# Four-layer graph network on one core: the second tile's record gather ahead of a semaphore clearing, and the relus of a slab ahead of the copies of the batch in front

## The chip, the cores and the metric

The kernel runs on one core of one Trainium2 chip. The metric is the device time of one execution in microseconds (us), as the median of several runs. Engines are called PE (TensorE; PEld its weight loads), DVE (VectorE), ACT (ScalarE), POOL (GpSimd) and SP (SyncE, which only issues transfers here). Each engine carries out its own instructions in order and waits on semaphores for the others.

## The reference

There are 2048 nodes with 512 features and 67584 edges sorted by destination. Four pre-norm layers are added to x one after another: graph attention with a bias by edge, a three-layer GCN, a single GCN layer, and a weighted sum over edges.

```python
h = relu(layernorm(x));  x = x + attention(h, edges, edge_attr)   # 32 graphs of 64 nodes, 8 heads
h = relu(layernorm(x));  x = x + gcn3(h, edges, W1..W3)
h = relu(layernorm(x));  x = x + gcn1(h, edges, W, b)
h = relu(layernorm(x));  x = x + relu(segment_sum((h @ weight)[dst] * edge_weight, src))
```

The attention needs, for each pair of nodes of a graph, the sum of the biases of the edges between them; the other layers need the counts and the weights of the edges as dense matrices. The change lies in the stage that builds these.

## The kernel before

The program has an edge stage (`edge_prep`, about the first 45 us), a build stage (`build_matrices`, up to about 440 us), the attention, and the three convolutions.

The edge stage packs each edge into a record of 11 fields in DRAM (`rec_dram`), computes the start index of each graph's records, normalizes x, and begins the transfers and projections of the build stage. Its semaphores form one block (`keep.prep`).

The build stage takes the records in 8 tiles (`GTILES`), t = 0 to 7. For each tile POOL issues two indirect transfers, z = 0 and 1, into the one buffer `gathered` (L718; those of tile 0 are at L241). PE transposes the 11 fields (`turn_fields`, L1128), which raises the semaphore `read` by 3 and so frees the buffer. ACT copies the fields from PSUM, DVE makes keys and ACT and DVE make two-part values of them. A tile is worked in 8 batches, so there are 64 batches, n = 8 t + i. Batch n is, engine by engine:

- DVE, `hots(n)`: one-hot matrices by comparison with iotas (L838, L841, L843), products with the weights (L851) and with the biases (L858). DVE works one batch ahead: in iteration n it issues hots(n+1), which waits until the matmuls of batch n-1 are done. In `hots(n+1)` it also issues `h_low` (L785) where batch n has node tiles to turn. Iteration 4 of a tile adds `prep_keys`, iteration 5 `residual` (L776, L777) for the next tile. `weight_low` (L822) makes the low parts of weights in iterations 1 to 3 and later ones.
- PE: the projection pieces that are put into this batch (L1183, L1166, 12 matmuls each), `turn_h` of node tiles (L1149), 32 matmuls for the biases (L1229, needs hots(n)), in the fourth batch of a tile `turn_fields(t+1)` (needs the gather of the next tile), then 32 short matmuls for counts and weights (L1240, L1241), and `turn_weights(n-4)` (L1140).
- ACT: the copies of the pieces, `copy_turned` (L1012) of node tiles, `copy_sums(n)` (L985 bias, fields of the next tile, L992 counts, L999 weights), `copy_weights(n-4)` (L980), parts of weights (`weight_high`, L1038), `relu(t)` (L1003, which reads a node tile of x that SP has loaded), and in the fourth batch of a tile `copy_part` (L967, L968).

Node tiles are turned in pairs, a slab. The first slabs are done at the start of the stage; later pairs are turned in batches 6, 12, 17, 22, 28 and 33. The relus that they need are issued in the batch in front of these: 5, 11, 16, 21, 27 and 32. Which batch holds which pieces is a fixed table (`projections`).

In `build_pool` the gathers of tile t wait for `read` to reach 3 t. Before the gathers of tile 1 POOL calls `clear_prep`, which waits until the last users of the edge stage's semaphores are through (among them `w_high`, raised by the four L1038 of batch 1) and clears them (L730).

Of the kernel before, what the change touches and what calls it, by code (L numbers as in the profile page):

```python
# [579 lines left out]
LAST = GTILES * NBATCH  # L580
# [41 lines left out]
def projections(first_round):  # L622

    pieces = {n: [] for n in range(LAST)}
    if not first_round:
        return pieces
    number, n = 0, SLAB_START  # L630

    def add(place, slab, parts):
        nonlocal number
        for c in parts:
            pieces[place].append(("q" if c < KT else "k", number, slab, c % KT))
            number += 1
    pieces["turns"], pieces["early"], pieces["start"] = [("h", 0), ("h", 1)], [], []
    add("early", 0, (0, 1))
    add("start", 0, (2, 3, 4, 5))
    pieces["start"].append(("total", 0))  # L640
    add(1, 0, (6, 7))
    pieces[1] += [("h", 2), ("h", 3)]
    for slab in range(1, SLABS):
        c = 0
        while c < 2 * KT:
            amount = 2 if slab == 1 else 1 if slab == SLABS - 1 and c >= KT else PIECES_OF_BATCH[n % NBATCH]
            take = range(c, min(c + amount, KT if slab == SLABS - 1 and c < KT else 2 * KT))
            add(n, slab, take)
            c = take.stop
            n += 1  # L650
        if slab + 1 < SLABS:
            pieces[n - 1] += [("h", 2 * slab + 2), ("h", 2 * slab + 3)]
    assert n <= V_START
    assert not any(piece[0] == "q" for b in range(min(b for b in HIGHS if 2 * KT in HIGHS[b]) + 1, V_START) for piece in pieces[b])
    pieces[SECOND_TOTAL].append(("total", 1))
    j, n = 0, V_START
    while j < 2 * NT:
        for _ in range(min(VALUES_OF_BATCH[n % NBATCH], 2 * NT - j)):
            pieces[n].append(("v", number, j // 2, j % 2))
            number += 1  # L660
            j += 1
        n += 1
    assert n < LAST
    return pieces


def work_slots(first_round):


    marks, uses = [], {}  # L670

    def use(key, mark):
        n = len(marks)
        uses[key] = n % WORK, marks[n - WORK] if n >= WORK else None
        marks.append(mark)
    pieces = projections(first_round)

    def use_pieces(place):
        for piece in pieces[place]:
            if piece[0] == "h":  # L680
                use(piece, ("h_copied" if piece[1] < 2 else "h_low", piece[1] + 1))
            elif piece[0] == "total":
                use(piece, ("w_read", 2 * piece[1] + 1))
            else:
                use(piece, ("projected", piece[1] + 1))
    if first_round:
        use_pieces("turns")
        use_pieces("early")
    for f in range(FGROUPS):
        use(("fields", 0, f), ("turned", f + 1))  # L690
    if first_round:
        use_pieces("start")
    for n in range(LAST):
        t, i = divmod(n, NBATCH)
        use_pieces(n)
        if t + 1 < GTILES and i == 3:
            for f in range(FGROUPS):
                use(("fields", t + 1, f), ("turned", FGROUPS * (t + 1) + f + 1))
        if n >= 4:
            use(("chunk", n - 4), chunk_mark(n - 4, first_round))  # L700
    for c in range(LAST - 4, LAST):
        use(("chunk", c), chunk_mark(c, first_round))
    return uses


def build_pool(nc, io, keep, m, s, first_round):

    pool = nc.gpsimd
    records = io["rec_dram"].rearrange("e f -> (e f)").unsqueeze(1)
    if not first_round:  # L710
        pool.wait_ge(s["indexed"], 1)
    for t in range(1 if first_round else 0, GTILES):
        if t > 0:
            pool.wait_ge(s["read"], FGROUPS * t)
        if first_round and t == 1:
            clear_prep(pool, keep, s)
        for z in range(2):
            pool.indirect_dma_start(keep.gathered[:, z, :], None, records,  # L718
                                    bass.IndirectOffsetOnAxis(ap=keep.idx[:, 2 * t + z:2 * t + z + 1], axis=0)).then_inc(s["got"], 16)


def clear_prep(pool, keep, s):

    pool.wait_ge(s["turned"], FGROUPS)
    pool.wait_ge(s["hots"], 1)
    pool.wait_ge(s["out_h"], 16)
    pool.wait_ge(s["w_high"], KT)
    nums = sorted(x.num for x in keep.prep.values())
    assert nums == list(range(nums[0], nums[0] + len(nums)))
    pool.sem_clear(range(nums[0], nums[-1] + 1))  # L730
# [212 lines left out]
def build_act(nc, io, keep, m, s, first_round, stage=None):  # L943

    act = nc.scalar
    uses, pieces = work_slots(first_round), projections(first_round)
    scale = float(HD) ** -0.5

    def copy_fields(t):
        for f in range(FGROUPS):  # L950
            bank, _ = uses["fields", t, f]
            n = min(4, FIELDS - 4 * f)
            act.wait_ge(s["read"], FGROUPS * t + f + 1)
            if t:
                act.wait_ge(s["parts"], part_count(t - 1, 0, first_round) if t > 1 else len(unit_parts(0, first_round)))
            act.copy(m.fields[:, 4 * f:4 * f + n, :],
                     m.work_ps[:, bank, 0:n * P].rearrange("p (f g) -> p f g", f=n)).then_inc(s["turned"], 1)
# [24 lines left out]
    def copy_sums(n):  # L982
        if first_round:
            act.wait_ge(s["bias_done"], n + 1)
            act.copy(keep.bias[:].rearrange("p (h t) m -> p t h m", h=H)[:, :, :, n],  # L985
                     m.bias_ps[:, 0:NT * H].rearrange("p (t h) -> p t h", h=H)).then_inc(s["biased"], 1)
        if n // NBATCH + 1 < GTILES and n % NBATCH == 3:
            copy_fields(n // NBATCH + 1)
        act.wait_ge(s["batch"], n + 1)
        if first_round:  # L990
            to_count = keep.count[:, :, :, n].rearrange("p s c (b h) -> p s c b h", h=2)
            act.copy(to_count, m.cw_ps[:, :, 0:CCOLS].rearrange("p (c b) (h s) -> p s c b h", c=GROUPS, h=2))  # L992
        q = n // 4
        if n % 4 == 0 and q >= 2:
            act.wait_ge(s["chunk"], 4 * (q - 1))
        if first_round and n == 4:
            act.wait_ge(s["w_low"], 2 * KT)
        slab = m.w_slab[:, q % 2, n % 4].rearrange("p (b c) -> p b c", b=BATCH)
        act.copy(slab, m.cw_ps[:, :, CCOLS:2 * CCOLS]).then_inc(s["slab"], 1)  # L999

    def relu(t):
        act.wait_ge(s[f"in_x{t % 2}"], 16 * (t // 2 + 1))
        act.activation(keep.h[:, t % 2], keep.h[:, t % 2], ACT.Relu, bias=keep.shift[:, t:t + 1],  # L1003
                       scale=keep.rstd[:, t:t + 1]).then_inc(s["relued"], 1)
# [20 lines left out]
    def weight_high(j):  # L1025
        if j % KT == 0:
            act.wait_ge(s["w_read"], 4 if j == 2 * KT else 2)
        if j == KT:
            act.wait_ge(s["proj"], 2 * KT)
            act.wait_ge(s["h_low"], 2)  # L1030
        if not KT <= j < 2 * KT:
            landed, value = part_landed(keep, j)
            act.wait_ge(landed, value)
        if j == 2 * KT:
            last = max(piece[1] for n in range(LAST) for piece in pieces[n] if piece[0] == "q")
            act.wait_ge(s["proj"], last + 1)
        which = j // KT
        act.activation(part_of(keep, j, 0), part_place(m, j), ACT.Copy, scale=keep.w_powers[:, which:which + 1]).then_inc(s["w_high"], 1)  # L1038
# [43 lines left out]
    for n in range(LAST):  # L1082
        t, i = divmod(n, NBATCH)
        for piece in pieces[n]:
            if piece[0] == "h":
                copy_turned(piece[1])
            elif piece[0] != "total":
                copy_projected(piece)
        if first_round and n == 1:
            for j in range(KT):  # L1090
                weight_high(j)
        copy_sums(n)
        if first_round and n in SQUARES:
            square_quarter(SQUARES[n])
        if first_round and n >= 4:
            copy_weights(n - 4)
        if first_round:
            for j in HIGHS.get(n, ()):
                weight_high(j)
        if n + 1 < LAST:  # L1100
            for piece in pieces[n + 1]:
                if piece[0] == "h" and n > 0:
                    relu(piece[1])
        if t + 1 < GTILES and i == 3:
            copy_part(t + 1)
    if first_round:
# [1654 lines left out]
```

## Time and profile before

| | |
|---|---|
| median of 3 runs | 1424.48 us (1424.43 to 1426.48) |
| profiled execution, its time | 1424.92 us |
| profiled execution, its span | 1423.7 us |
| PE busy | 1367.0 us, 96% |
| DVE busy | 888.0 us, 62% |
| ACT busy | 568.8 us, 40% |
| POOL busy | 86.1 us, 6% |

PE is busy for nearly the whole span and carries 85% of the chain that ended last. The slices of the page show where it isn't: the first three, of some 36 us each, have PE at 7, 8 and 6 tenths. The times in the rows below count from the start of the span, whose end lies 1.2 us under the execution's own time.

### The profile page before, as it was taken

The page shows a single profiled execution, that of the slowest core. Times are in us where ns is not written, and L with a number is a line of the kernel's source. Part 1 is how long each engine was busy: PE and PEld are TensorE (multiplying, and loading weights), DVE is VectorE, ACT ScalarE, POOL GpSimd, SP SyncE. Part 2 cuts the span into 40 slices and gives each one's busy share as a digit, 9 for nine tenths or more (in the row PEclk, how much of TensorE's full clock was granted, in tenths as well). Part 3 has the DMA queues.
Part 4 walks back from the last instruction along what each step waited for, and adds up shares of the span by engine and source line. Part 5 has one row for each costly group of instructions (what it writes and reads, how often), then busy time and mean ns, then how long its engine had stood idle before and what let it go on. Part 6 is the DMA issues. An engine that isn't in the chain of part 4 may idle for free.

```text
span 1423.7 us, 26665 instructions
## 1 busy us (share of the span) xinstructions
PE 1367.0 (96%) x11273; PEld 844.7 (59%) x11273; DVE 888.0 (62%) x1382; ACT 568.8 (40%) x977; POOL 86.1 (6%) x86
## 2 busy tenths in 40 slices
PE   7869999989997999999999999999999999999998
PEld 7759888889996665544444444444444445444443
DVE  6979898999996887666664766542344232532322
ACT  2646566565654447611133112412243224432322
POOL 3050000000001220000000100002200000000000
PEclk9989999999997999999999999999999999999999
DMA  9534343444447661200000100012202222553201
GB/s 336 195 97 135 125 141 125 138 130 140 147 135 244 192 205 38 84 30 0 1 1 7 53 1 0 0 31 81 82 15 60 60 75 66 214 207 104 90 0 59
DMA packets 71331, 136.90 MB, mean 96 GB/s; under 512 B 11908, under 2 KB 24324, under 8 KB 69798
## 3 DMA queue, kind: packets, MB, share of 16 engines
q1 hardware_dynamic: 68542, 123.98, 26.5%
q0 software_dynamic: 1280, 5.77, 1.6%
q10 hardware_dynamic: 1384, 5.38, 1.0%
q8 instruction: 91, 1.49, 0.4%
q14 instruction: 34, 0.28, 0.1%
HBM read 81.79 MB, written 53.32 MB: 95 GB/s over the span
## 4 chain that ended last, share of the span: by engine, by line
PE 85%; DVE 7%; ACT 4%; DMA 2%; issue 2%; POOL 0%; ACTq 0%; POOLq 0%; DVEq 0%
PE banks L2268 31%; PE banks L2202 13%; PE banks L2332 11%; PE banks L1229 6%; PE banks L1618 3%; PE banks L1183 3%; PE banks L1166 3%; PE banks L1240 2%; PE banks L1140 2%; DVE x_sb L858 2%; DMA gathered<-rec_dram,idx 1%; PE banks L2146 1%; PE banks L1588 1%; PE banks L1577 1%; PE banks L1241 1%
## 5 line engine op out<-in xcount | busy, mean ns | idle before, releaser
L2268 PE MATMUL banks<-g,count 128*128 128x512 f16 x1024 | 227.6, 379 | 0.5 <-DVE tiles L2534 0.5
L2268 PE MATMUL banks<-count,g 128*128 128x512 f16 x1024 | 223.6, 379 | 0.0
L2202 PE MATMUL banks<-w_parts,h_parts 128*128 128x512 f16 x960 | 215.3, 379 | 1.4 <-DVE g L2483 1.1
L2268 PEld LDWEIGHTS banks<-count,g 128*128 128x128 f16 x1024 | 99.6, 98 | 118.1
L2268 PEld LDWEIGHTS banks<-g,count 128*128 128x128 f16 x1024 | 99.7, 98 | 113.5 <-DVE tiles L2534 1.0
L2332 PE MATMUL banks<-g,part 128*128 128x512 f16 x768 | 165.9, 379 | 0.0
L2202 PEld LDWEIGHTS banks<-w_parts,h_parts 128*128 128x128 f16 x960 | 91.2, 98 | 115.1 <-issue 11.9
L858 DVE TENSOR_TENSOR x_sb<-eb_parts,x_sb 128x4096 f16<-128x4096 f16 x64 | 146.0, 2281 | 0.0
L1229 PE MATMUL banks<-x_sb 128*128 128x128 f16 x2048 | 128.0, 222 | 12.6 <-DVE x_sb L858 12.6
L1229 PEld LDWEIGHTS banks<-x_sb 128*128 128x128 f16 x2048 | 121.9, 99 | 15.7 <-DVE x_sb L858 14.5
L2332 PEld LDWEIGHTS banks<-g,part 128*128 128x128 f16 x768 | 75.1, 98 | 90.6
L2615 DVE SCALAR_TENSOR_TENSOR part<-count,e_scale,part 128x1024 f16<-128x1024 f32 x29 | 37.2, 1284 | 105.9 <-ACT part L2099 105.9
L2073 ACT ACTIVATE h_gcn_t<-h_gcn_t,b_col,unscale 128x512 f32<-128x512 f32 x32 | 26.0, 813 | 169.2 <-DVE h_gcn_t L2526 169.2
L843 DVE TENSOR_TENSOR x_sb<-iota_src,keys 128x2048 f16<-128x2048 f16 x64 | 77.7, 1215 | 0.0
L2099 ACT ACTIVATE part<-count,e_scale 128x1024 f16<-128x1024 f32 x29 | 33.3, 1148 | 110.9 <-PE banks L2332 110.9
L2422 DVE TENSOR_TENSOR h_parts<-h_gcn_t,h_parts 128x512 f16<-128x512 f32 x48 | 39.7, 829 | 48.4 <-ACT h_parts L1982 48.3
L1240 PE MATMUL banks<-x_sb 128*128 128x64 f16 x1024 | 66.0, 191 | 0.0
L1241 PE MATMUL banks<-x_sb 128*128 128x32 f16 x1024 | 65.0, 179 | 0.0
L1240 PEld LDWEIGHTS banks<-x_sb 128*128 128x128 f16 x1024 | 61.6, 98 | 0.5
L2483 DVE SCALAR_TENSOR_TENSOR g<-banks,g_scale,g 128x512 f16<-128x512 f32 x64 | 47.6, 747 | 22.1 <-ACT g L2005 21.9
L1241 PEld LDWEIGHTS banks<-x_sb 128*128 128x128 f16 x1024 | 59.9, 96 | 0.1
L1618 PE MATMUL banks<-wo_sb,att_t 128*128 128x512 f32 x128 | 57.9, 595 | 0.4 <-ACT att_t L1522 0.4
(339 smaller groups left out, 1901.1 us busy)
## 6 DMA issues: line engine op xcount, KB each, us to landing
weight_dram<-w_new SPq DMA_DIRECT2D x62, 256.0 KB, 2.6
count<-weight_dram SPq DMA_DIRECT2D x29, 512.0 KB, 7.0
qk_dram<-stage SPq DMA_DIRECT2D x64, 128.0 KB, 2.4
tiles<-x_dram SPq DMA_DIRECT2D x32, 256.0 KB, 3.5
x_dram<-tiles SPq DMA_DIRECT2D x32, 256.0 KB, 2.8
count<-in_x SPq DMA_DIRECT2D x4, 1024.0 KB, 11.7
h<-in_x SPq DMA_DIRECT2D x16, 256.0 KB, 5.0
h_dram<-h_t SPq DMA_DIRECT2D x8, 512.0 KB, 3.0
```

Source lines behind the costliest of these rows:

```text
L843: dve.tensor_tensor(m.hot_src[:, z].rearrange("p g (c two) -> p g c two", two=2), keep.iota_src[:].rearrange("p (c two) -> p c two", two=2 ...
L858: dve.tensor_tensor(m.hot_eb[:, z].rearrange("p g (t c) -> p g t c", t=NT), values, tiles, ALU.mult).then_inc(s["hots"], 1)
L1166: mm = pe.matmul(out, m.h_slab[slab % 2][:, zh, k, tile * P:(tile + 1) * P], keep.wq[:, zw, k, c * SCOLS:(c + 1) * SCOLS], start=n == 0, s ...
L1183: mm = pe.matmul(out, weights[:, zw, k, cols], m.h_t[:, zh, k, :], start=n == 0, stop=n == len(passes) - 1)
L1229: mm = pe.matmul(m.bias_ps[:, 0:NT * H], m.hot_src[:, z, g], parts[:, part], start=g == part == 0, stop=g == BATCH - 1 and part == 1)
L1240: pe.matmul(m.cw_ps[:, g, 0:2 * CCOLS], m.hot_src[:, z, g], m.hot_cw[:, z, g, 0:2 * CCOLS], start=True, stop=False)
L1241: mm = pe.matmul(m.cw_ps[:, g, CCOLS:2 * CCOLS], m.hot_src[:, z, g], m.hot_cw[:, z, g, 2 * CCOLS:CW], start=False, stop=True)
L1618: mm = pe.matmul(m.wo_ps[:, t % 2], m.att_t[:, k, :], keep.wo[:, k, :], start=k == 0, stop=k == KT - 1)
L2202: mm = pe.matmul(out, m.h_parts[:, slot, zh, k], m.w_parts[:, zw, k], start=n == 0 and layer != 3, stop=n == len(passes) - 1)
L2268: mm = pe.matmul(m.agg_ps[:, b], lhs, rhs, start=i == 0 and z == 0, stop=i == NT - 1 and z == 1)
L2332: mm = pe.matmul(m.banks[:, b], m.part[:, n % 3, z, b * P:(b + 1) * P], m.g[:, q, gz], start=q == 0 and (z, gz) == (0, 0), stop=q == NT - ...
L2483: dve.scalar_tensor_tensor(lo, result, scale, hi, ALU.mult, ALU.subtract).then_inc(s["glo"], 1)
```

## The change

Two statements change their place; no instruction is added, removed or changed in size. In `build_pool` the call of `clear_prep` goes behind the two gathers of tile 1. In `build_act` the relus that batch n issues for the slab of batch n+1 go ahead of `copy_sums(n)`.

```diff
@@ build_pool
         if t > 0:
             pool.wait_ge(s["read"], FGROUPS * t)
-        if first_round and t == 1:
-            clear_prep(pool, keep, s)
         for z in range(2):
             pool.indirect_dma_start(keep.gathered[:, z, :], None, records,
                                     bass.IndirectOffsetOnAxis(ap=keep.idx[:, 2 * t + z:2 * t + z + 1], axis=0)).then_inc(s["got"], 16)
+        if first_round and t == 1:
+            clear_prep(pool, keep, s)
@@ build_act
         if first_round and n == 1:
             for j in range(KT):
                 weight_high(j)
+        if n + 1 < LAST:
+            for piece in pieces[n + 1]:
+                if piece[0] == "h" and n > 0:
+                    relu(piece[1])
         copy_sums(n)
         if first_round and n in SQUARES:
             square_quarter(SQUARES[n])
@@
         if first_round:
             for j in HIGHS.get(n, ()):
                 weight_high(j)
-        if n + 1 < LAST:
-            for piece in pieces[n + 1]:
-                if piece[0] == "h" and n > 0:
-                    relu(piece[1])
         if t + 1 < GTILES and i == 3:
             copy_part(t + 1)
```

## Rows read from the trace of the kernel before

**Rows 1.** Chain of waits, 40 to 104 us: start, duration, what.

```profile
68.77 2.46 ACT wq_sb L1038 x4
...
75.24 18.19 DMA gathered<-rec_dram,idx
```

**Rows 2.** Timeline of PE, 40 to 104 us; in brackets the idle time before.

```profile
51.41 1.49 PE L1128 MATMUL banks<-ident,gathered 128*128 128x128 f32 x11
...
74.17 3.36 PE L1229 MATMUL banks<-x_sb 128*128 128x128 f16 x32 [3.42 <-DVE x_sb L858]
...
82.62 1.96 PE L1229 MATMUL banks<-x_sb 128*128 128x128 f16 x32 [1.60 <-DVE x_sb L858]
93.48 2.62 PE L1128 MATMUL banks<-ident,gathered 128*128 128x128 f32 x11 [8.90 <-DMA gathered<-rec_dram,idx]
```

**Rows 3.** Timeline of POOL: the gathers of tiles 1, 2 and 3.

```profile
72.40 2.54 POOL L718 DMA_INDIRECT gathered<-rec_dram,idx  x1 [25.73 <-issue]
75.24 15.41 POOL L718 DMA_INDIRECT gathered<-rec_dram,idx  x1 [0.30 <-issue]
96.37 0.95 POOL L718 DMA_INDIRECT gathered<-rec_dram,idx  x1 [5.72 <-PE banks L1128]
97.63 1.03 POOL L718 DMA_INDIRECT gathered<-rec_dram,idx  x1 [0.31 <-issue]
...
143.00 0.96 POOL L718 DMA_INDIRECT gathered<-rec_dram,idx  x1 [0.30 <-issue]
```

**Rows 4.** Timeline of DVE, 40 to 104 us.

```profile
52.48 0.17 DVE L406 SCALAR_TENSOR_TENSOR shift<-stats,rstd 128x12 f32<-128x12 f32 x1
...
54.74 0.42 DVE L767 SCALAR_TENSOR_TENSOR keys<-fields,ints 128x256 bf16<-128x256 f32 x1
...
66.19 0.16 DVE L807 COPY w_small<-banks 128x2 f32<-128x2 f32 x1
...
71.84 2.27 DVE L858 TENSOR_TENSOR x_sb<-eb_parts,x_sb 128x4096 f16<-128x4096 f16 x1
74.04 1.27 DVE L785 TENSOR_TENSOR h_t<-banks,h_t 128x512 f16<-128x512 f32 x2
...
88.43 1.39 DVE L822 SCALAR_TENSOR_TENSOR wk_sb<-w_slab,w_small,wk_sb 128x512 f16<-128x512 f32 x2
97.42 0.42 DVE L838 TENSOR_TENSOR x_sb<-iota_cnt,keys 128x512 f16<-128x512 f16 x1 [7.59 <-PE banks L1241]
```

**Rows 5.** Chain of waits, 94 to 145 us: the biases of batch 7.

```profile
117.42 1.79 PE banks L1229 x32
```

**Rows 6.** Timeline of DVE, 102 to 145 us: the end of hots(7).

```profile
113.17 1.29 DVE L785 TENSOR_TENSOR h_t<-banks,h_t 128x512 f16<-128x512 f32 x2 [0.28 <-ACT h_t L1012]
114.37 2.28 DVE L858 TENSOR_TENSOR x_sb<-eb_parts,x_sb 128x4096 f16<-128x4096 f16 x1
```

**Rows 7.** Waits of PE, 94 to 433 us: in total, times, longest.

```profile
PE banks L1229 <- DVE x_sb L858: 7.6, 4, 2.9
PE banks L1149 <- ACT h L1003: 3.5, 5, 0.7
PE banks L1183 <- DVE h_t L785: 1.6, 2, 0.8
```

**Rows 8.** ACT: the relus of batch 11 (timeline), and its longest wait up to 640 us.

```profile
143.92 1.52 ACT L1003 ACTIVATE h<-h,shift,rstd 128x512 f32<-128x512 f32 x2
...
ACT bias L985 <- PE banks L1229: 79.4, 56, 4.9
```

**Rows 9.** Timelines of DVE and PE, 145 to 186 us: behind these relus.

```profile
148.78 1.29 DVE L785 TENSOR_TENSOR h_t<-banks,h_t 128x512 f16<-128x512 f32 x2 [3.90 <-ACT h_t L1012]
...
165.27 3.06 PE L1229 MATMUL banks<-x_sb 128*128 128x128 f16 x32 [1.97 <-DVE x_sb L858]
```

**Rows 10.** Transfers of x: issues of one pair (SP), and all on the page.

```profile
114.85 1.26 SPq L1267 DMA_DIRECT2D h<-in_x  x2
...
h<-in_x SPq DMA_DIRECT2D x16, 256.0 KB, 5.0
```

## The prediction

> **What bounds the kernel now.** I read the page first: PE is busy 96% of the span and carries 85% of the chain that ended last, so only a place where PE waits can give time back. The slices put most of PE's idle time into the edge and build stages. The chain of waits, read from 40 to 104 us, shows a long piece that isn't PE: ACT's parts of Wq end at 71.23, POOL clears and issues, a gather is under way from 75.24 for 18.19 us, and then PE turns the fields of tile 1 [rows 1]. PE's timeline prices it: its work of batch 3 stops at 84.58 (82.62 + 1.96) and goes on at 93.48, an idle time of 8.90, the longest in the stage [rows 2]. POOL's timeline says why the data are late: the first gather of tile 1 is issued at 72.40, though PE had read tile 0's fields at 52.90 (51.41 + 1.49) and POOL's other gathers of the stage start 0.27 us behind that read (93.48 + 2.62 = 96.10, issue at 96.37). What lies between is the clearing's wait for the last L1038 [rows 1 to 3].
>
> From 94 to 433 us PE waits for three things only: 7.6 us in 4 waits for DVE's L858, 3.5 us in 5 waits for ACT's relus, 1.6 us in 2 waits for DVE's L785 [rows 7]. The relu waits are about 0.7 each, one before each turned pair of batches 12, 17, 22, 28 and 33. That of batch 6 has none.
>
> **The gather.** New start of the first gather of tile 1: 52.90 + 0.27 = 53.17. It needs 0.95 to 1.03 us of POOL where nothing holds it [rows 3], so it ends at about 54.1, and the second begins 0.30 later, at 54.4. The second gather of the old place didn't take 1 us but 15.41, so I have to know what held it. It ends at 90.65; DVE's work without a gap ends at 89.82 (88.43 + 1.39), 0.83 before. The first one ends at 74.94, and DVE's L858 ended at 74.11 (71.84 + 2.27), again 0.83 before [rows 3, 4]. So DVE holds it. But it isn't any DVE work: the first ended while L785 ran (from 74.04, two of them, one input from PSUM), and those at 97.63 and 143.00 took 1.03 and 0.96 beside short comparisons that had just begun. From 75.24 to 89.82 each DVE instruction (L822, L838 to L858) reads two SBUF tensors. I take it that a run of such instructions keeps the descriptor work out, and an instruction with fewer SBUF inputs lets it in.
>
> At the new place DVE is idle from 52.65 (52.48 + 0.17) to about 53.7, where the first gather passes. The second meets the small key operations, then from 54.74 L767 and the first two batches' one-hots, without a break until L807 at 66.19, a copy from PSUM, with eight tiny operations of one input behind it [rows 4]. Best case: it ends at 55.4. Worst case under this reading: held until 66.3, it ends 0.83 later, at 67.2. The old one's data had landed 2.8 us after its POOL work (93.44 against 90.65) [rows 1, 3]; so they are there by 70, when PE asks at 84.58. Both cases give the same: the wait of 8.90 is gone, with over 14 us of cover.
>
> The rows show that DVE's two-input instructions and a gather don't go together. The Trainium skill says so too (SBUF — State Buffer, Who interferes with whom): a DVE instruction with two SBUF inputs shuts out a GpSimd instruction that reads SBUF, and whoever issued first keeps the ports. By that rule the new place is safe as above. The same section adds that copies, casts and tensor_scalars in a two-port mode shut out the writing of descriptors; by that alone the second gather would lose a few tenths near 54.5, no more.
>
> What is late next is DVE. PE at 84.58 turns the fields (1.40), does the counts of batch 3 (0.86) and would be 8.9 us early, or 10.7 with what it lost at half clock behind the idle time (L1128 2.62 instead of 1.40, the like behind it). DVE gains less: hots(5) waited for the counts of batch 3 until 97.42 [rows 4]. Now these are done at 86.84, but DVE itself is busy until 89.74 with L822. So it gains 7.68. From 97.42 DVE worked on without a break to 112.88, then waited 0.28 for ACT [rows 6]; that too goes, as PE and ACT come earlier than DVE. hots(7) ended at 116.65 (114.37 + 2.28); it now ends at 116.65 - 7.68 - 0.28 = 108.69. PE, with 1.31 of a piece behind batch 6, is there at 106.7, waits 2.0, and starts the biases of batch 7 at 108.7 instead of 117.42 [rows 5]. Gain of the gather: 8.7. Behind it PE needs more per batch than DVE (DVE idles several times from 94 on), so PE leads again and keeps 8.7.
>
> The clearing now runs when `w_high` allows, as before, with nothing behind it on POOL until the gathers of tile 2, due after 86. It costs nothing. The gathers' 160 packets (0.72 MB) now share the DMA engines with Wk, x and Wq from 53 to 60, at about 400 GB/s: 1.8 us of delay at most. PE's first users of Wk may slip by some tenths, but PE waits 3.42 and 1.60 us for DVE behind that [rows 2]; cost 0.
>
> **The relus.** The two take 1.41 us of ACT (1.52 less an overlap of 0.1) [rows 8]. Ahead of `copy_sums(n)` they fall into the time in which ACT waits for the bias matmuls (1.79 us long): ACT waited there 56 times, 79.4 us in all [rows 8]. At worst they push the bias copy by 0.2, and it is not asked for until the next batch's biases; the three field copies of batches 11 and 27 slip by the same and end just as the counts begin. Price: nothing, and if that cover were gone, 0.2 us at each of six places, 1.2. The x tiles are there: the pair for batch 12 was issued from 114.85 on, lands in about 5, and is read at 139 instead of 143.92 [rows 8, 10]. The gain is the five waits of 0.7: 3.5 [rows 7]. At batches 12 and 28 `copy_part` (2.5 us) stood between the relus and the copies of the turned tiles; all of it now ends 1.4 earlier, so DVE's L785, which waited 3.90 for ACT, comes 1.4 earlier (148.78 to 147.37) [rows 9], and PE's L1183, which waited 0.8 for it, is 1.4 ahead in all: 0.7 more at each of the two. Some batches later PE waits for hots(15) [rows 9] and for its like of tile 3; DVE's run up to these starts at that L785, so they come 1.4 earlier as well and the gain lasts. The waits for DVE near 308 have an idle DVE ahead that follows PE. Sum: 3.5 + 1.4 = 4.9.
>
> **The clock.** A bias group took 3.06 us behind an idle time of 1.97 and 3.36 behind 3.42, but 1.96 behind 1.60 [rows 2, 9]; the new wait of 2.0 at batch 7 lies between. Half clock there costs 1.1, or nothing. I take half of it, 0.5.
>
> **Sum:** 8.7 + 4.9 - 0.5 = 13.1 us. The profiled execution would go from 1424.92 (span 1423.7) to 1411.8, and the median, which lies 0.44 below it, to 1411.4. Bounds: without clock loss, and with a full 1.8 lost behind the old gather given back, 15; with the relus' gain gone or halved and 1.2 of cost, 8.
>
> **Rivals.**
> 1. The second gather is held until DVE is wholly idle, as the end at 89.82 also allows. DVE has no such time between 53.66 and 89.82, so the data land at 93.4 again. The old first gather's end beside L785 speaks against it. It leaves the relus: 4.9, so 1419.6.
> 2. PE's waits for DVE take more: each relu wait saved turns up again at a wait for L858, as DVE's operations per batch (4.6 us, and 3.8 more per tile) are close to PE's 4.5 to 5.8. DVE's idle 3.90 speaks against it. Only the gather counts: 1415.8.
> 3. Half clock falls in new places or the new wait at batch 7 comes again at others, 3 us in all: 1414.
> 4. Slower: the relus wait for x ahead of `copy_sums(n)` and hold the bias and weight copies, which PE needs. The decisive point is the landing of a pair: at batch 11 it must come 24 us after its issue, when about 5 is the measured time [rows 10]. At six places it would have to hold ACT by 2.8 us each to eat the 13.1 and 3 more: 1427.5.
> 5. Nothing moves, because both waits hide another transfer or engine just as late: 1424.5.
>
> **Chances.** Forecast (gain 12 to 14.5) 0.62; more than that 0.05; rival 3, a gain of 9.5 to 12, 0.14; rival 2, 0.07; rival 1, 0.07; rival 5, 0.03; rival 4, 0.02. The range goes from 1409.0 to 1416.0: it takes in rivals 2 and 3 and leaves out 1, 4, 5 and a little of the top. The measurement of this kernel can tell about 0.2% (2.9 us) from no change. By these cases faster by more is 0.95, within it 0.03, slower 0.02.
>
> **What would show it.** In the new profile: L718 at about 53.2 and again near 54.4, the second ending by 67.2; no wait of L1128 for the gather; a new wait of about 2 us of PE's L1229 for L858 near 107, with the biases of batch 7 at 108.7; L1003 directly ahead of L985, no wait of L1149 for it; L785 of batch 12 near 138.7 (147.37 less 8.7). Wrong would make me: a second gather with some 35 us on POOL; L985 or L992 that start late and PE waiting for them; PE's waits for L858 well above the 7.6 us plus 2.

## The result and the profile after

The changed kernel takes 1411.7 us (median of 4 runs, 1410.82 to 1412.54) against 1425.48 us of the kernel before on the same chip (4 runs, 1424.43 to 1427.12): a ratio of 0.9902, 95% interval 0.9885 to 0.9919, so 13.8 us less. Forecast were 1411.4 us and a gain of 13.1. The profiled execution took 1412.54 us, its span 1411.3.

The page of the changed kernel, its head and busy times:

```profile
span 1411.3 us, 26665 instructions
PE 1363.5 (97%) x11273; PEld 843.0 (60%) x11273; DVE 886.9 (63%) x1382; ACT 568.5 (40%) x977; POOL 78.7 (6%) x86
```

PE does the same 11273 matmuls in 12.4 us less span. POOL is busy 7.4 us less although it issues the same transfers; why, its timeline tells (changed kernel, 40 to 130 us; start, duration, what, idle time before and what ended it):

```profile
55.12 0.94 POOL L716 DMA_INDIRECT gathered<-rec_dram,idx  x1 [6.66 <-PE banks L1128]
56.37 0.98 POOL L716 DMA_INDIRECT gathered<-rec_dram,idx  x1 [0.30 <-issue]
88.16 9.62 POOL L716 DMA_INDIRECT gathered<-rec_dram,idx  x1 [30.81 <-ACT fields L956]
98.08 1.16 POOL L716 DMA_INDIRECT gathered<-rec_dram,idx  x1 [0.30 <-issue]
```

The two gathers of tile 1 stood at 72.40 and 75.24 and took 2.54 and 15.41 [rows 3]; now they take 0.94 and 0.98 and start 17.3 and 18.9 us earlier. Those of tile 2, which had taken about 1 us each, are now the ones in trouble: one takes 9.62. It costs nothing, as PE asks for these data only at 133. A time of this trace lies 1.91 us late against before, all of it from the edge stage (the biases of batch 0 start at 62.50 instead of 60.59, after a transfer of edge attributes that took 7.79 instead of 6.25 us). That is no effect of the change: in the traces of all runs this start lies anywhere from 59.95 to 63.80, whatever the edit. Where times of two kernels are compared below, they are counted from the start of the biases of batch 0, which takes this out.

PE's timeline of the changed kernel around the place of the old wait, then around batch 7:

```profile
84.53 1.96 PE L1229 MATMUL banks<-x_sb 128*128 128x128 f16 x32 [1.50 <-DVE x_sb L858]
86.33 1.56 PE L1128 MATMUL banks<-ident,gathered 128*128 128x128 f32 x11
...
106.37 0.69 PE L1140 MATMUL banks<-ident,w_slab 128*128 128x128 f32 x4
108.43 1.47 PE L1183 MATMUL banks<-h_t,wq_sb 128*128 128x256 f16 x12 [1.37 <-DVE h_t L785]
110.54 1.96 PE L1229 MATMUL banks<-x_sb 128*128 128x128 f16 x32 [0.64 <-DVE x_sb L858]
```

The fields of tile 1 are turned without a wait, in 1.56 instead of 2.62 us [rows 2]. The new wait of about 2 us at batch 7 is there, in two pieces: 1.37 for DVE's L785 ahead of the piece, 0.64 for its L858 behind it.

PE's waits of the changed kernel, 80 to 425 us (us in total, times, longest):

```profile
PE banks L1229 <- DVE x_sb L858: 10.6, 7, 3.0
PE banks L1183 <- DVE h_t L785: 2.5, 3, 1.4
PE banks L1140 <- ACT w_slab L999: 0.7, 1, 0.7
```

The line of L1149 for ACT's relus, 3.5 us in 5 waits [rows 7], is gone. ACT's timeline of the changed kernel shows the new order ahead of batch 12, with the relus in front of the bias copy:

```profile
132.39 1.53 ACT L1003 ACTIVATE h<-h,shift,rstd 128x512 f32<-128x512 f32 x2
133.80 0.40 ACT L985 COPY bias<-banks 128x128 f32<-128x128 f32 x1
133.97 1.52 ACT L956 COPY fields<-banks 128x512 f32<-128x512 f32 x3
...
137.62 2.12 ACT L968 ACTIVATE eb_parts<-fields,scale 128x1024 f16<-128x1024 f32 x1
139.62 0.57 ACT L1052 ACTIVATE stage<-banks,bk_col,w_small 128x256 f32<-128x256 f32 x1
140.07 1.09 ACT L1012 CAST h_t<-banks 128x512 f16<-128x512 f32 x2
```

and DVE's timeline of the same kernel what comes of it:

```profile
140.71 1.29 DVE L785 TENSOR_TENSOR h_t<-banks,h_t 128x512 f16<-128x512 f32 x2 [2.52 <-ACT h_t L1012]
```

L785 waited 3.90 [rows 9], now 2.52. Between the relus and L1012 the two parts (L967, L968, 2.5 us) still stand; the best experiment below starts from there.

### The profile page after: what moved, and what is told of

Read it like the earlier page. It is cut to its first block, busy times and chain, and to the rows that moved or that the text cites. A ratio compares the mean times of both kernels' runs of the same rounds, so it can differ in the third digit from the quotient of the medians.

```text
span 1411.3 us, 26665 instructions
## 1 busy us (share of the span) xinstructions
PE 1363.5 (97%) x11273; PEld 843.0 (60%) x11273; DVE 886.9 (63%) x1382; ACT 568.5 (40%) x977; POOL 78.7 (6%) x86
## 4 chain that ended last, share of the span: by engine, by line
PE 82%; DVE 12%; ACT 2%; issue 2%; DMA 1%; ACTq 0%; DVEq 0%
PE banks L2268 31%; PE banks L2202 13%; PE banks L2332 11%; PE banks L1229 6%; PE banks L1618 3%; DVE x_sb L858 3%; PE banks L1166 3%; PE banks L1183 2%; PE banks L1240 2%; PE banks L1140 1%; DVE x_sb L843 1%; PE banks L2146 1%; PE banks L1588 1%; PE banks L1606 1%; PE banks L1577 1%
## 5 line engine op out<-in xcount | busy, mean ns | idle before, releaser
L858 DVE TENSOR_TENSOR x_sb<-eb_parts,x_sb 128x4096 f16<-128x4096 f16 x64 | 145.8, 2279 | 0.0
L1229 PE MATMUL banks<-x_sb 128*128 128x128 f16 x2048 | 127.6, 221 | 14.1 <-DVE x_sb L858 14.0
L1229 PEld LDWEIGHTS banks<-x_sb 128*128 128x128 f16 x2048 | 121.4, 99 | 17.8 <-DVE x_sb L858 16.7
```

The lines of the kernel that those rows point to most:

```text
L858: dve.tensor_tensor(m.hot_eb[:, z].rearrange("p g (t c) -> p g t c", t=NT), values, tiles, ALU.mult).then_inc(s["hots"], 1)
L1229: mm = pe.matmul(m.bias_ps[:, 0:NT * H], m.hot_src[:, z, g], parts[:, part], start=g == part == 0, stop=g == BATCH - 1 and part == 1)
```

## Experiments

Medians are compared with the kernel before in the same job, on the same chip. Three jobs were run. In the second and third, before took 1425.67 and 1426.54 us; in the first it took 1430.58 (17 runs), and all four kernels of that job show long waits of ACT's L992 that no other trace has: 2.3 to 2.5 us in batches 11 and 43, put down to "remote", and 1.7 in batches 19, 27 and 35. This is the one of batch 11 in ACT's timeline of the gather moved alone:

```profile
135.31 0.58 ACT L992 CAST count<-banks 128x512 f16<-128x512 f32 x1 [2.38 <-remote]
```

DVE's L838 starts in the same instant, 135.31, after a wait of 3.12. Both wait for the count matmuls of the batch, the last of which ended at 133.16; in the third job's run of the same kernel L992 started 0.03 behind that matmul's end. So what came late seems to be PE's signal, and not ACT's own work. The recorded expectations speak of two such waits, in batches 11 and 27. The first job's small differences are not used, and its two halves were run again in the third. The first job has no trace of the kernel before; where its traces are set against before, that is the trace whose rows stand ahead of the prediction.

A ledger by batch serves for all. It has the start of the bias matmuls (L1229) of batch n in PE's timeline, counted from that of batch 0, before minus the kernel named (the two halves are those of the third job, the last row is from the second):

```
batch                       4      7     12     16     17     22     29     33     63
changed kernel          10.72   8.62   9.75   9.97  11.12  12.27  13.39  14.53  14.91
gather alone            10.72   8.60   8.59  10.07  10.07  10.07  10.07  10.07   9.81
relus alone             -0.02   0.22   1.37   3.07   4.22   5.38   6.50   7.64   8.02
parts a batch later     10.72   8.62   9.76  13.56  14.71  15.50  17.61  20.12  20.49
```

**1. The gather alone** (first job). POOL's part of the change, without the relus.

```diff
-        if first_round and t == 1:
-            clear_prep(pool, keep, s)
         for z in range(2):
...
+        if first_round and t == 1:
+            clear_prep(pool, keep, s)
```

> Only the gather of tile 1 moved ahead of the clearing, the relus where they were. My theory: the gather is worth 8.7 us of the sum, so the time is 8.7 under the kernel before, or 9.3 if the half clock near 309 us of the old trace goes with it; the five relu waits of 0.7 before L1149 and two of 0.8 before L1183 are still there. Rival (the waits for DVE take back what the gather gives): under 6 us.

Measured: 1422.47 us (5 runs), ratio 0.9947 (0.9934 to 0.996), 8.1 us less. No wait of L1128 is left, but at batch 12 the trace is only 6.06 ahead of before's, while the same kernel's trace in the third job is 8.59 ahead: the other 2.5 went with the wait of 2.38 at L992.

**2. The relus alone** (first job). The other half.

```diff
+        if n + 1 < LAST:
+            for piece in pieces[n + 1]:
+                if piece[0] == "h" and n > 0:
+                    relu(piece[1])
         copy_sums(n)
...
-        if n + 1 < LAST:
-            for piece in pieces[n + 1]:
-                if piece[0] == "h" and n > 0:
-                    relu(piece[1])
```

> Only the relus moved; the clearing stays ahead of the gather. My theory: 4.9 us under the kernel before; the wait of L1128 for the gather stays at 8.9, the five waits of L1149 are gone, the two of L1183 shrink. Rival (the relus only pay once the gather is early, or their gain turns up again as a wait for L858): under 2 us.

Measured: 1429.06 us (12 runs), ratio 0.9983 (0.9974 to 0.9991), 1.5 us less. This looked as if the relus brought next to nothing (rival 2). PE's waits, 80 to 430 us, do have what rival 2 foretold: no L1149 for the relus, but other waits in their place.

```profile
PE banks L1229 <- DVE x_sb L858: 10.9, 7, 2.9
PE banks L1128 <- DMA gathered<-rec_dram,idx: 9.0, 1, 9.0
PE banks L1183 <- DVE h_t L785: 2.5, 3, 0.9
PE banks L1149 <- ACT w_new L980: 2.5, 2, 1.6
```

The last line stands in the relu variants of this job alone, 2.5 us in two waits, behind the waits at L992 of batches 11 and 27.

**3. The gather in the middle of the one-hots** (first job). The changed kernel, with tile 1's gathers made to wait until hots(0) is done, so that they meet DVE's run of batch 1.

```diff
+        if first_round and t == 1:
+            pool.wait_ge(s["hots"], 1)
         for z in range(2):
...
```

> The changed kernel, with POOL's gathers of tile 1 waiting in addition for hots(0), so that they are asked for near 62.5 us, in the middle of DVE's unbroken run of two-input instructions. My theory: the first is held until L807 (near 68.1) and ends 0.83 later, near 69; the second starts 0.3 later and ends between 72 and 77, at L869 or L785, which read PSUM and one SBUF tensor; its data land before 80, so PE at 86 doesn't wait and the time is that of the changed kernel within 1 us. Rival (POOL is held until DVE is wholly idle, which it is only at about 91.7 us): the second ends near 92.5, its data land at 95.3, PE waits about 9 us and the time is some 9 us longer.

Measured: 1419.37 us (4 runs), ratio 0.9922 (0.9908 to 0.9936). POOL's timeline:

```profile
61.51 5.82 POOL L718 DMA_INDIRECT gathered<-rec_dram,idx  x1 [14.71 <-DVE x_sb L860]
67.63 0.94 POOL L718 DMA_INDIRECT gathered<-rec_dram,idx  x1 [0.30 <-issue]
```

The first is held, and ends at 67.33: 0.83 us behind the end of L860 at 66.50 (L858 of before), which a copy from PSUM follows. The 0.83 is the same as in [rows 3, 4]. So the worst case of the prediction, a hold until the copy from PSUM and an end near 67.2, was made to happen, and it cost PE nothing: there is no wait for the gather in this trace. The second gather was expected to be held until 72 to 77; it took 0.94 and ended at 68.57.

**4. Less DVE work ahead of batch 7** (first job). The changed kernel, with the four low parts of Wk set to zero by a memset instead of computed; the low half of Wk is left out of the projections.

```diff
+        if which == 1:
+            dve.memset(part_of(keep, j, 1), 0.0).then_inc(s["w_low"], 1)
+            return
```

> The changed kernel with the four L822 of batches 2 and 3 (the low halves of Wk) replaced by DVE memsets to zero, so that the low part of Wk is left out of the products: DVE has about 1.8 us less to do between the gather's old place and hots(7). My theory (DVE is what is late next, by 2.0 us, at batch 7): PE's waits of 1.37 and 0.64 before batch 7's pieces and biases shrink to under 0.6 together, and the time falls by 1.4 to 1.9 us. Rival (PE's wait there comes from ACT's copy of the turned tiles): the waits stay at 2.0 and the time does not move.

Measured: 1418.96 us (5 runs), ratio 0.9911 (0.9898 to 0.9924). PE's timeline at batch 7:

```profile
108.20 1.47 PE L1186 MATMUL banks<-h_t,wq_sb 128*128 128x256 f16 x12
110.14 1.96 PE L1232 MATMUL banks<-x_sb 128*128 128x128 f16 x32 [0.47 <-DVE x_sb L861]
```

The 1.37 is gone and 0.47 is left of 0.64. Against before this trace is 10.32 us ahead at batch 7, the third experiment's 8.50. So DVE was the late one there, and its lateness is worth 1.8 us at that place. At the end of the build stage 1.2 of it is left (9.37 against 8.14), and the medians, 0.4 apart, don't separate it; that the time falls by the 1.4 to 1.9 expected is not shown.

**5. The kernel before and the change again** (second job), to see what belongs to the first job.

> The kernel before, unchanged, for a profile from the chip of this job. In the first four runs ACT's L992 of batches 11 and 27 waited 2.35 us each for something that neither profile of the first chip shows. My theory: that wait belongs to the chip or its loading and not to the edits, so this profile shows it too and with it relu waits of 2 to 3 us before L1149 of batches 12 and 28. Rival: it comes with the edits, and this profile does not show it.

> The changed kernel, unchanged, on the chip of this job. If L992 of batches 11 and 27 waits 2.35 us as in the first four runs, I expect some 11 to 12 us under the kernel before, as with the gather put into the one-hots; without these waits 13 to 14.

Measured: before 1425.33 us (one execution); the change 1412.36 us (4 runs), ratio 0.9903 (0.9888 to 0.9918), 13.3 us less. Neither has a long wait at L992. So those waits come neither from the kernel before nor from the edits. What they are stays open.

**6. The parts a batch later** (second job). The changed kernel, with `copy_part` of the next tile in the fifth batch of a tile instead of the fourth, which takes its 2.5 us out from between the relus and L1012 in batches 11 and 27.

```diff
-        if t + 1 < GTILES and i == 3:
+        if t + 1 < GTILES and i == 4:
             copy_part(t + 1)
```

> The changed kernel with copy_part moved from the end of a tile's fourth batch to the end of its fifth, so that in batches 12 and 28 ACT copies the turned tiles 2.5 us earlier. My theory: after the change DVE's L785 of these batches waits for exactly this copy (2.5 us), PE's L1183 of batches 13 and 29 and its biases of batches 15 and 31 wait for DVE in turn (0.6 and 2.0), so each of the two places gives up to 2.5 us and the time is 3 to 5 us under the changed kernel. Rival (DVE is bound over the whole tile by the sum of its own work, not by the late copy): under 1 us. Rival (residual of the next tile now waits for copy_part): slower.

Measured: 1405.83 us (4 runs), ratio 0.9864 (0.9849 to 0.9879): 19.8 us under before and 6.5 under the change in the same job, more than was expected. DVE's timeline for L785 of batch 12, and PE's for the biases of batch 15:

```profile
136.05 1.29 DVE L785 TENSOR_TENSOR h_t<-banks,h_t 128x512 f16<-128x512 f32 x2 [0.43 <-ACT h_t L1012]
```

```profile
152.54 1.96 PE L1229 MATMUL banks<-x_sb 128*128 128x128 f16 x32 [0.60 <-DVE x_sb L858]
```

In the changed kernel the second was

```profile
157.20 3.11 PE L1229 MATMUL banks<-x_sb 128*128 128x128 f16 x32 [1.97 <-DVE x_sb L858]
```

The wait of 1.97 shrinks to 0.60, and the matmuls behind it take 1.96 instead of 3.11, at a granted clock of 1.00 where the changed kernel's was 0.52. In the ledger the step from batch 12 to 16 is 3.80 against 0.22 of the change: 0.7 from PE's wait at batch 13, 1.4 from the wait at 15, 1.5 from the clock. In batches 29 and 31 the same two waits get shorter again, without a change of the clock. At the end of the build stage this is 5.6 more than the change (20.49 against 14.91), 4.1 without the clock, which is what was expected.

**7. One instruction of one input** (second job). The kernel before, with a one-column copy from SBUF to SBUF behind L822 of batch 1, in the middle of the run in which the second gather is held. It tests the wording of the prediction, that an instruction with fewer SBUF inputs lets it in.

```diff
                 weight_low(j)
+            if n == 1:
+                dve.tensor_copy(m.ints[:, 0, 0:1], m.ints[:, 1, 0:1])
```

> The kernel before with nothing moved: one DVE copy of a single int32 column is added behind the low parts of batch 1, near 78 us, in the middle of the run of two-input instructions that held the second gather of tile 1 for 15.4 us. My theory: that gather gets in at this copy and ends about 0.83 us later, near 79 instead of 90.6; its data land near 82, before PE asks at 84.6; so nearly the whole gain of the moved gather, 7.5 to 9 us, comes from an instruction of under 0.2 us. Rival (POOL needs DVE wholly idle, or is held by something else, such as the clearing): no change, and POOL's second L718 still takes 15 us.

Measured: 1426.51 us (11 runs), ratio 1.0005 (0.9996 to 1.0015). Timeline of POOL, then of DVE at the copy:

```profile
73.20 2.53 POOL L718 DMA_INDIRECT gathered<-rec_dram,idx  x1 [26.26 <-issue]
76.04 15.47 POOL L718 DMA_INDIRECT gathered<-rec_dram,idx  x1 [0.31 <-issue]
```

```profile
78.68 0.13 DVE L937 COPY ints<-ints 128x1 int32<-128x1 int32 x1
78.75 0.40 DVE L838 TENSOR_TENSOR x_sb<-iota_cnt,keys 128x512 f16<-128x512 f16 x1
```

Nothing moves. The wording is wrong: such an instruction doesn't let the gather in.

**8. The same copy with a wait behind it** (third job). DVE waits for its own copy before it goes on.

```diff
             if n == 1:
-                dve.tensor_copy(m.ints[:, 0, 0:1], m.ints[:, 1, 0:1])
+                dve.tensor_copy(m.ints[:, 0, 0:1], m.ints[:, 1, 0:1]).then_inc(s["dve"], 1)
+                k += 1
+                dve.wait_ge(s["dve"], k)
```

> The kernel before with the same one-column copy as in the run that changed nothing, at the same place near 78.7 us, but DVE now waits on a semaphore until this copy is done, before it goes on. In all traces POOL's held gathers got on 0.83 us before their end where DVE had a gap of at least 0.02 us (the clearing of the run after 89.8, the wait in prep_keys) or passed to an instruction that reads PSUM. Theory A (a gap is enough): the second gather of tile 1 ends near 79.6 instead of 91.5, PE's wait for it is gone, and the time falls by 7.5 to 9 us. Theory B (only an instruction that reads PSUM, or a long idle time, lets it in): 15.4 us again and no change.

Measured: 1415.89 us (4 runs), ratio 0.9923 (0.9908 to 0.9938), 10.7 us less. Timeline of POOL, then of DVE:

```profile
74.98 3.54 POOL L718 DMA_INDIRECT gathered<-rec_dram,idx  x1 [0.30 <-issue]
```

```profile
77.62 0.13 DVE L937 COPY ints<-ints 128x1 int32<-128x1 int32 x1
77.79 0.43 DVE L838 TENSOR_TENSOR x_sb<-iota_cnt,keys 128x512 f16<-128x512 f16 x1
```

The copy starts 0.17 us ahead of L838, not 0.07 as without the wait; from its end at 77.75 to L838 there is a gap of 0.04. That is enough: the gather ends at 78.52, and PE's wait for it is gone. The point 0.83 before that end is 77.69, where the L822 ahead of the copy ends. So it is the wait that lets the gather in, but the 0.83 leads to the start of the copy, not to the gap, which lies 0.77 before the gather's end. A wait of a few hundredths of a microsecond on DVE is worth what the move of the gather is worth.

**9. An instruction that reads PSUM in the run** (third job). The kernel before, with the second of the two `h_low` of batch 1 (L785, one input from PSUM, the other from SBUF) behind the L822 instead of ahead of them. No instruction and no wait on another engine is added.

```diff
             h_low(2)
-            h_low(3)
         if first_round:
             for j in LOWS.get(n, ()):
                 weight_low(j)
+            if n == 1:
+                h_low(3)
```

> The kernel before with no instruction added: of the two L785 of batch 1, which read PSUM and one SBUF tensor, the second goes behind the four L822, to about 78.1 us, into the run that held the second gather. If an instruction that reads PSUM lets a held gather in, as L785 at 74.04 did in the trace of before, the second gather ends near 79 and the time falls by 7.5 to 9 us. If it needed the end of the run, 15.4 us again and no change.

Measured: 1416.03 us (4 runs), ratio 0.9927 (0.9912 to 0.9942), 10.5 us less. Timeline of POOL, then of DVE:

```profile
76.20 2.94 POOL L718 DMA_INDIRECT gathered<-rec_dram,idx  x1 [0.30 <-issue]
```

```profile
77.59 0.73 DVE L822 SCALAR_TENSOR_TENSOR wq_sb<-w_beside,w_small,wq_sb 128x512 f16<-128x512 f32 x1
78.25 0.67 DVE L785 TENSOR_TENSOR h_t<-banks,h_t 128x512 f16<-128x512 f32 x1
78.85 0.40 DVE L838 TENSOR_TENSOR x_sb<-iota_cnt,keys 128x512 f16<-128x512 f16 x1
```

The gather ends at 79.14, 0.82 behind the end of L822 at 78.32. DVE has no gap there; what comes next is the instruction with its input in PSUM.

**10. Both halves again** (third job), with the edits of experiments 1 and 2.

> The gather alone once more, since the first chip job had two waits of 2.35 us on ACT (L992 of batches 11 and 27) that the second did not show. Without them I expect 8.7 to 9.3 us under the kernel before, the five relu waits of 0.7 unchanged.

> The relus alone once more. Without the two ACT waits of 2.35 us I expect 4 to 5 us under the kernel before. If it stays near 2.4 as in the first job, the relus pay less than the five waits and two half waits, because DVE's waits before batch 23 and later ones grow.

Measured: the gather alone 1415.3 us (5 runs), ratio 0.9927 (0.9913 to 0.994), 11.2 us less; the relus alone 1418.37 us (5 runs), ratio 0.9942 (0.9929 to 0.9956), 8.2 us less. Both are above what was expected (8.7 to 9.3, and 4 to 5). Together 19.4, where the whole change gains 13.8. The ledger says where: 8.60 for the gather at batch 12, in both the half and the whole, and 6.0 for the relus (batches 12, 17, 22 and 23, 28 and 29, 33) in both. But from batch 15 to 16 each half gains 1.46 that the whole doesn't. There before and the changed kernel have a stretch of 3.4 us with a granted clock of 0.53 and 0.52 (at 166.1 before, 157.9 after), and in the halves it is 1.00. The second traces of before and of the change have the slow stretch too, and the traces of experiments 6, 8 and 9 don't, so that the 10.7 and 10.5 of experiments 8 and 9 contain these 1.46 as well. 9.81 + 8.02 - 14.91 = 2.92, twice 1.46. The other 2.7 us lie outside the build stage or in the spread between executions.

## Why the prediction was right

**The gather, 8.7 forecast, 8.6 measured.** Each step has its row. The first gather was to start at 53.17 and the second at 54.4; less the 1.91 they stand at 53.21 and 54.46. The wait of 8.90 is gone. The biases of batch 7 were to start at 108.7: 110.54 less 1.91 is 108.6. That DVE and not PE sets this point, experiment 4 shows: with less DVE work 1.8 us more come back. PE keeps the gain from there, as the ledger's 8.60 from batch 7 to 12 of the gather alone shows.

**The hold: right where it was used, wrong in its wording.** That DVE's run held the gather was right, and the best of the two cases came about: the second gather took 0.98. But the rule taken ("an instruction with fewer SBUF inputs lets it in") fell in experiment 7. What the runs show in its place stands below, and it has exceptions. It didn't matter, as both cases of the prediction left over 14 us of cover; experiment 3 made the worse one and PE didn't wait. Rival 1, a hold until DVE is wholly idle, is out: in experiment 9 the gather ends with DVE busy throughout.

**The relus, 4.9 forecast, 5.9 measured in the changed kernel and 6.0 alone.** The mechanism was right, the term was sized too small. Each of the five places was priced with the wait that the page shows, 0.69. In the ledger a place gives 1.15. In before's PE timeline the piece L1183 of batch 12 starts at 142.72, the pair L1149 at 144.89, the biases at 146.05; without the wait the first distance is 1.31 instead of 2.17, which makes 0.86 where the idle time reads 0.69, and the second is 0.29 shorter (the second of the pair waited a little too, and its 8 matmuls took 1.33 us instead of 1.04). Five times 1.15 is 5.8, to which batches 13, 23 and 29 add and subtract a quarter each. The 0.7 more that were foreseen at the two places with `copy_part` came only as 0.25: L785 came 1.4 earlier against PE's biases of batch 11, but PE itself came 1.15 earlier by then, so its wait for L785 shrank from 0.8 to 0.57 and no more. So the errors stood against each other, 2.3 too little at the five places, 0.9 too much at the two, and 0.25 lost at batch 23 that wasn't foreseen. L785 of batch 12 was to start near 138.7: 140.71 less 1.91 is 138.8.

**The clock, -0.5 forecast.** At batch 7 it cost nothing: the bias group behind the new wait took 1.96, and its wait is two short ones. One stretch at half clock went away instead: the biases at 308.07 took 2.55 behind 2.94 of idle time before, and take 1.96 at 295.45 behind 2.95 now, 0.38 in the ledger. But that isn't the change's doing: in the second trace of the changed kernel the same group took 3.33 behind 2.94, and the ledger loses 0.35 there, so this term differs from one execution to the next. The forecast put its loss at batch 7, and none came there. The sum by the trace is 8.6 + 5.9 + 0.4 = 14.9 at the end of the build stage. The profiled span shows 12.4, as 1.91 were lost in the edge stage and 0.6 behind the build stage; the medians show 13.8, between the two. That they come within 0.7 of the forecast is in part luck: the trace's sum lies 1.8 above it, by 1.0 in the relus and 0.9 in the clock, and 2.5 was lost outside the build stage, which nobody forecast.

**The rivals.** 1 and 5 are out by the traces above. 2 showed in the first job only, where the long waits at L992 made ACT late again; the ledger of the third job has no trace of it, and from 88 to 425 us PE waits 9.1 us for L858, no more than the 7.6 plus 2 allowed (the 10.6 above has 1.50 more from 84.53, ahead of the stretch of [rows 7]). 3 is what separates the halves from the whole, 1.46 at one place, and stood in before as well. 4, relus that wait for x, didn't occur: L1003 runs without idle time ahead of L985.

**Open.** Why the stretch at batch 15 is at half clock in before and the changed kernel but not in the halves, when PE's idle time ahead of it is alike (1.97): the traces show the same wait with either outcome. And why ACT and DVE, in the first job, started some 2.1 us behind PE's count matmuls in five batches.

## What to carry to other kernels

When a small transfer issued by POOL takes ten times its usual POOL time, look at what DVE runs beside it before you look at the queue: a gap, or an instruction with an input in PSUM, at the right place in DVE's order can be worth as much as moving the transfer (10.5 us of 1426 here, by one swapped call). Price a wait by the distance between the starts of the work around it, not by the idle time shown alone: here 1.15 us against 0.69. And when a wait is shortened, look at once for what else stands in the same chain: taking `copy_part` from between the relus and L1012 gave another 6.5 us.

## What the runs showed of the hardware

**What holds a gather on POOL and what lets it go.** The traces of all runs have 26 gathers that took more than 1.2 us on POOL. Each ends 0.81 to 0.83 us behind the end of a DVE instruction. In nine cases the next instruction reads PSUM (L785 in before, with its first gather, and in experiment 9; a copy from PSUM in experiment 3). In five DVE falls idle (89.82 in before). Nine are alike, the 9.62 us one of the changed kernel among them, which ends at 97.78: the chain of waits of that kernel shows DVE 0.83 before, between two small key operations.

```profile
96.34 0.14 DVE ints L756
96.48 0.20 DVE fields L758
96.68 0.14 DVE ints L760
96.82 0.15 DVE ints L761
96.96 0.02 issue
96.99 0.23 DVE match L764
```

It isn't let in at L756, L760 or L761, casts and tensor_scalars with one SBUF input, nor at the copy of experiment 7. It is let in at 96.95, at the 0.02 of a semaphore wait. The wait ahead of L760, which leaves no gap, doesn't do it. So the number of SBUF inputs is not what counts. DVE itself was not slowed by more than 0.03 us (L858 took 2.27 to 2.30 us, with a held gather beside it or without).

Three cases are left. One is the copy of experiment 8. One is in experiment 4: the gather ends at 91.68, 0.82 behind the end of an L861 (L858 of before) at 90.86, where a memset starts at once; it has no PSUM input. The third has neither a gap nor PSUM. It is the first gather of tile 2 in experiment 8, in POOL's timeline:

```profile
86.18 3.07 POOL L718 DMA_INDIRECT gathered<-rec_dram,idx  x1 [7.66 <-PE banks L1132]
```

It ends 0.82 behind the end of L858 at 88.43, and what had begun at 88.34 is an L822 that works from SBUF to SBUF. So an instruction that reads PSUM, or a gap by a semaphore wait, let the gather in wherever one came up in the run; that nothing else does is not so, and a rule for all 26 isn't found.

The Trainium skill (SBUF — State Buffer, Who interferes with whom) says that a DVE instruction in a two-port mode shuts out the writing of descriptors, copies, casts and tensor_scalars among them. That copies and casts don't release the gather doesn't contradict it; whether they ran in such a mode no run shows. By the same section of the Trainium skill a tensor_tensor was not seen to stall such a transfer, though with two SBUF inputs it contends with what GpSimd reads; in experiment 3 DVE ran nothing but tensor_tensors while the first gather was held (61.51 to 66.42), so here the measurement decides.

Not explained: gathers that are issued within about 1 us behind a gap of DVE, as at 97.63 before and 98.08 after, take 1.03 and 1.16 although two-input comparisons are already under way.

**The clock behind a wait.** Equal idle times of PE had either outcome in these traces: 2.94 and 2.95 us ahead of a group of 32 matmuls that took 2.55 in before and 1.96 in the changed kernel, and 3.33 behind 2.94 in a second trace of the changed kernel. Behind 1.97 or 1.96 at batch 15 it took 3.06 in before and 3.11 in the changed kernel, and 1.96 in both halves; the slow stretch had a granted clock of 0.53 and 0.52, close to the lower level of 1.2 GHz, the other one 1.00, which is 2.4 GHz.
